# Projecting Q and K of the next head pair inside the attention loop, with two score regions instead of three

## The reference

```python
x = L0_attn_x                                     # (8, 2048, 1024) float32
x = x + attn(layernorm(x), W_qkv, W_out)
x = x + ffn(layernorm(x), w1, b1, w2, b2)

# attn: 16 heads of 64, W_qkv (16, 1024, 192), W_out (16, 64, 1024)
q, k, v = split(einsum('bsd,ndh->bnsh', x, W_qkv), 3)
attn = softmax(einsum('bnqh,bnkh->bnqk', q, k) / 8 + causal_mask)
out = einsum('bnqk,bnkh->bnqh', attn, v).reshape(B, -1, S)
return einsum('bds,nhd->bsd', out, W_out)         # 'h' and 'n' of W_out are summed away
# ffn: relu(x @ w1 + b1) @ w2 + b2, width 4096
```

## Time and profile before

| what | us |
|---|---|
| runs without the profiler | 1423.0 and 1475.0 (median 1449.0) |
| the profiled execution | 1413.5 |
| its span on the slowest core (core 7) | 1412.0 |
| spans of the other cores | 1388.7 to 1406.0 |
| mean granted clock of PE, by core | 0.886 to 0.898 of full |
| PE busy on core 7 | 1005.7 (71%) |
| DVE busy | 531.2 (38%) |
| ACT busy | 363.5 (26%) |
| eight head pairs, first QK matmul to last PV | about 608 |

### The profile page before, as it was taken

The page is one execution under the profiler, slowest core; times in us unless marked ns, Lnnn a source line. Parts: engine busy times, 40 slices in busy tenths (PEclk is TensorE's granted clock), DMA queues, the critical chain, the costliest instruction groups (busy, mean ns, idle before and its releaser), DMA issues.

```text
span 1412.0 us, 12665 instructions; the slowest of 8 cores (1388.7 to 1412.0 us)
## 1 busy us (share of the span) xinstructions
PE 1005.7 (71%) x4656; PEld 392.9 (28%) x4656; DVE 531.2 (38%) x686; ACT 363.5 (26%) x395; POOL 101.0 (7%) x131
## 2 busy tenths in 40 slices
PE   1155677758675866768575638798879887998797
PEld 0022332212221221212121113343334432443343
DVE  0545442362617162534536273222323232313301
ACT  0000007557392928464664700000000000000000
POOL 2100020000000000000000000111011101110110
PEclk9988998988798988989898859898999988999999
DMA  9900062010101000110002007879697949796976
GB/s 243 116 0 0 1 56 20 5 11 1 16 1 15 1 1 1 13 17 1 1 0 31 0 0 108 129 115 186 86 139 120 190 72 132 126 182 108 131 125 140
DMA packets 94331, 93.17 MB, mean 66 GB/s; under 512 B 40000, under 2 KB 72768, under 8 KB 94272
## 3 DMA queue, kind: packets, MB, share of 16 engines
q0 software_dynamic: 85248, 75.57, 38.6%
q1 hardware_dynamic: 9024, 16.80, 3.9%
HBM read 159.54 MB, written 8.39 MB: 119 GB/s over the span
## 4 chain that ended last, share of the span: by engine, by line
PE 60%; DVE 18%; DMA 12%; issue 4%; ACT 3%; DVEq 2%; POOL 0%; ACTq 0%; POOLq 0%
PE arena L667 16%; PE arena L622 12%; PE arena L478 11%; DMA wstage<-w 9%; PE arena L366 7%; PE arena L423 6%; PE arena L286 5%; DVE tmp_sb L550 4%; DVE oscr_sb L495 3%; DVE x_sb L561 3%; DMA wstage<-wout 2%; DVEq L51 2%; PE arena L438 2%; PE arena L239 1%; ACT p_sb L451 1%
## 5 line engine op out<-in xcount | busy, mean ns | idle before, releaser
L451 ACT ACTIVATE p_sb<-arena,cst_sb 128x1024 bf16<-128x1024 f32 (+1 forms) x320 | 288.9, 983 | 140.2 <-PE arena L438 134.0
L622 PE MATMUL arena<-lnf_sb,wstage 128*128 128x512 bf16 x1024 | 249.1, 408 | 64.0 <-DMA wstage<-w 53.6
L478 PE MATMUL arena<-p_sb,vaug_h 128*128 128x512 bf16 (+3 forms) x640 | 187.8, 378 | 131.8 <-DVE oscr_sb L495 96.2
L667 PE MATMUL arena<-w2stage,h_sb 128*128 128x512 bf16 x1024 | 221.7, 379 | 4.0 <-DVE h_sb L635 4.0
L635 DVE TENSOR_SCALAR h_sb<-arena,b1c_sb 128x512 bf16<-128x512 f32 x128 | 96.1, 751 | 215.0 <-PE arena L622 215.0
L622 PEld LDWEIGHTS arena<-lnf_sb,wstage 128*128 128x128 bf16 x1024 | 104.6, 103 | 207.6 <-issue 105.9
L366 PE MATMUL arena<-lnf_sb,wstage 128*128 128x512 bf16 x512 | 128.8, 412 | 36.8 <-DVE kpair L387 30.9
L667 PEld LDWEIGHTS arena<-w2stage,h_sb 128*128 128x128 bf16 x1024 | 99.9, 98 | 125.8 <-issue 5.9
L423 PE MATMUL arena<-qpair,kpair 64*128 64x512 bf16 (+3 forms) x640 | 123.0, 381 | 13.1 <-DVE kpair L387 13.1
L495 DVE COPY oscr_sb<-arena 128x512 f32<-128x512 f32 x64 | 44.3, 692 | 219.6 <-PE arena L478 214.7
L203 ACT ACTIVATE rsd_sb<-bag_sb,cst_sb 128x4 f32<-128x4 f32 x8 | 2.4, 300 | 457.1 <-DVE bag_sb L199 457.1
(11 more groups left out here) (37 smaller groups left out, 453.2 us busy)
## 6 DMA issues: line engine op xcount, KB each, us to landing
wstage<-w POOLq DMA_DIRECT2D x32, 1024.0 KB, 11.1
w2stage<-w POOLq DMA_DIRECT2D x64, 512.0 KB, 7.1
x_sb<-x SPq DMA_DIRECT2D x4, 2048.0 KB, 24.8
y<-y_sb SPq DMA_DIRECT2D x16, 512.0 KB, 6.5
wstage<-wqkv POOLq DMA_DIRECT2D x24, 256.0 KB, 12.3
wstage<-wout POOLq DMA_DIRECT2D x4, 512.0 KB, 21.2
b1c_sb<-b SPq DMA_DIRECT2D x32, 0.5 KB, 6.9
identb_sb<-identf POOLq DMA_DIRECT2D x1, 32.0 KB, 8.5
```

The costliest lines, as they stand in the source:

```text
L451: e.activation(AP(p_sb, (si_ % 3) * 1024, [[3 * 1024, 128], [512, 2], [1, w_]]), AP(arena, b_ + off_, [[AR, 128], [512, 2], [1, w_]]), AF. ...
L478: e.matmul(AP(arena, (4 + hx) * 512 + off_, [[AR, 128], [1, w_]]), vaug_h[:, hx, j_ * 128:(j_ + 1) * 128], AP(p_sb, (si_ % 3) * 1024 + hx ...
L622: (lambda s_, dc_, fb_, wp_: lambda e: e.matmul(bankap(fb_, TF), AP(wstage, s_ * 1024 + dc_ * 512 + wp_ * 128, [[8 * 1024, 128], [1, 128]] ...
L667: (lambda s_, ww_, c2_, dh_, t_: lambda e: e.matmul(bankap(t_, 512), h1_sb[:, ww_, 128 * c2_:128 * (c2_ + 1)], w2stage[:, s_, 512 * dh_:51 ...
```

## The change

Four things change, all in the attention stage.

- Q and K of pair n+1 are projected during the steps of pair n. `make_qk_chunks` cuts the projection into 8 chunks, each of 8 matmuls and two DVE copies. A chunk is added after PV(i) and its epilogue, where `npv % 5 == 2`: after PV(1), PV(6), PV(11), PV(16), PV(21), PV(26), PV(31) and PV(36). `qpair` and `kpair` have two halves, one for each parity of the pair. Only pair 0 is projected ahead of its own steps, as before.
- Banks 0 and 1 belong to the chunks alone. The scores have two regions instead of three, and the loop keeps two steps ahead instead of three. PE's queue in a pair is S(0), S(1), PV(0), S(2), PV(1), chunk, S(3), PV(2), and so on.
- The two V copies of a pair and the permute of the pair before now follow each other on DVE with nothing between them. The weight loads of a pair are issued one pair earlier.
- `onorm_sb` is bf16 instead of float32: written by L515, read by the strided multiply L550.

The core of the diff:

```diff
-        qpair = asb("qpair", [128, S], BF16)
-        kpair = asb("kpair", [128, S], BF16)
+        qpair = asb("qpair", [128, 2, S], BF16)
+        kpair = asb("kpair", [128, 2, S], BF16)
-        onorm_sb = asb("onorm_sb", [64, 2, S], F32)
+        onorm_sb = asb("onorm_sb", [64, 2, S], BF16)
...
-        s_reg_free = [("ex", 0)] * 3
-        REG_BASE = [1024, 3072, 0]
+        s_reg_free = [("ex", 0)] * 2
+        REG_BASE = [1024, 3072]
...
+        def make_qk_chunks(pi, slots_):
+            pr = pi % 2
+            chunks = []
+            for hix in range(2):
+                sl, dwqk = slots_[hix]
+                for g in range(4):
+                    def chunk(sl=sl, dwqk=dwqk, hix=hix, g=g):
+                        qb2 = g % 2
+                        mm_last = None
+                        for dcc in range(DC):
+                            w0 = ([dwqk, ("vv", vv_lnf1),
+                                   qk_bank_free[qb2]] if dcc == 0 else [])
...
+                        if g == 3:
+                            slot_free[sl] = ("mm", mm_last)
...
+                        qk_bank_free[qb2] = ("vv", vvk)
+                        vv_qk_pair[pi] = vvk
+                    chunks.append(chunk)
+            return chunks
...
+            if npair == 0:
+                for ch in make_qk_chunks(0, load_pair_slots(heads)):
+                    ch()
...
+            if npair + 1 < NH // 2:
+                next_chunks = make_qk_chunks(
+                    npair + 1,
+                    load_pair_slots((2 * npair + 2, 2 * npair + 3)))
+            else:
+                next_chunks = []
+            vv_qk_done = vv_qk_pair[npair]
             if pending_permute is not None:
                 perm_done = pending_permute()
                 pending_permute = None
...
-                reg = si % 3
+                reg = si % 2
...
             while npv < len(steps):
-                if nse < len(steps) and nse - npv < 3:
+                if nse < len(steps) and nse - npv < 2:
                     emit_se(nse)
                     nse += 1
                 else:
...
                     npv += 1
+                    if nck < len(next_chunks) and npv % 5 == 2:
+                        next_chunks[nck]()
+                        nck += 1
```

## The result

The changed kernel is slower. Its runs have a median of 1462.6 us (10 runs) against 1412.0 us for the kernel before (9 runs); the ratio is 1.035, with a 95% interval of 1.031 to 1.039. The prediction had 1441 on the profiled execution's scale, a ratio of 1.019, and put 1445 us on record. So the sign of its sum was right and its size was about half: +27 us forecast, +49 us by the ratio.

A forecast was written before the change was run, and what follows sets the result against it. The prediction took DVE to bound each pair's head and ACT its body. Its terms, -96.6 + 74 + 44 + 6 + 0 = +27 us on 1413.5, gave 1441, recorded as 1445 us on a 1418 scale, range 1415 to 1480.

The forecast's parts named there:

- Part 1: Head of each pair: without the QK block PV(4) starts earlier, 13.6 us in pairs 1 to 6, 15.0 in pair 7; -96.6 us.
- Part 2: Body: ACT idles about 1.6 us behind each exposed chunk, 10.3 us a pair in 7 pairs, 2 in pair 0; +74 us.
- Part 3: Body with two score regions: steps 1.13 us apart against 1.00 and costlier epilogues, 5.5 us a pair; +44 us.
- the walk of the prediction: Blocks 2 and 3 with two regions, summed link by link: 16.0 us against 14.6, and 20.5 against 17.1.
- Part 4: PE's clock: a half-clock stretch may follow the thin start of block 3; bounds 0 and 20, taken as +6 us.
- Part 5: onorm_sb in bf16: the permute's strided multiply L550 keeps its 1.89 us; 0 us, bounds -21 and +21.
- Rival A: Body: the chunks vanish in its slack, sum -40 us, 1378 us on the 1418 scale; chance 0.12.
- Rival C: PE's clock: half clock at the start of the three blocks behind an epilogue, +60 us instead of 6, 1499; chance 0.08.

The follow-up runs named there:

- a_nochunk: The changed kernel with pairs 0 and 1 projected up front and the later pairs' projections left out; 1397.4 us, ratio 0.986.
- b_two_fill: b_two with 6 matmuls that nobody reads behind each of PV(11), PV(12), PV(23) and PV(24); 1477.1 us, ratio 1.043.
- b_two: The kernel before with two score regions and two steps ahead, nothing else changed; 1505.3 us, ratio 1.063.
- a_both: The changed kernel with the permute spread behind two epilogues and chunks placed in PE's waits, two ahead of PV(0); 1299.9 us, ratio 0.916.
- b_spread: The kernel before with the permute moved out of the head, half behind each epilogue of blocks 1 and 2; 1355.1 us, ratio 0.954.
- a_both_la3: a_both with three steps ahead of the PV matmuls instead of two; 1241.8 us, ratio 0.874.

## Why the prediction was wrong, step by step

The prediction added up five parts. Its sum was +27 us, and measured were +49 by the ratio and +51.3 in spans. The term that failed is that of the two regions, Parts 3 and 4: forecast 50 us, measured 85 to 93.

**Part 1, the head: right.** Forecast 13.6 us in pairs 1 to 6 and 15.0 in pair 7. From copy to copy it is 13.6 to 14.8 in pairs 1 to 6 (34.6 - 20.9 = 13.7 in pair 5) and 15.1 in pair 7 (35.0 against 19.9), together 99.5 against the 96.6 forecast.

**Part 2, the chunks: the mechanism right, the price a sixth too high.** Forecast 10.3 us a pair in the body and 1.4 in the head; measured against `a_nochunk`, 8.5 and 1.4 in pair 5, and 8.9 in the blocks on average. The idle of 1.62 us behind a chunk is as forecast. Block 3 costs the forecast 4.8. The difference is mostly in block 2 (2.0 against 3.2), where the chunk behind PV(11), forecast as free, also keeps the clock up: 1.00 with chunks, 0.81 in `a_nochunk`.

**Part 3, two regions: the step that failed, in block 1.** In `b_two_fill` the clock is 1.00 in blocks 2 and 3, so it shows the walk of the prediction without the clock: 16.1 and 20.6 us, where the walk gave 16.0 and 20.5. For block 2 the 14.6 that it was compared with was the wrong base, for it held a stretch at the low clock. Against the 13.6 of the even pairs the chain costs 2.4 us and not 1.4. Block 1 was not walked. The prediction gave it +0.7, with the argument that PE is the bound there in both kernels. Over eight pairs it is 13.4 us in `b_two` against 10.3, +3.1; in pair 5 it is +3.4. The changed kernel's timeline shows what the argument missed:

```profile
560.44 1.01 PE L504 MATMUL arena<-p_sb,vaug_h 128*128 128x512 bf16 x2 [9.04 <-DVE oscr_sb L521]
561.39 0.61 PE L449 MATMUL arena<-qpair,kpair 64*128 64x512 bf16 x2
561.51 1.15 ACT L533 ACTIVATE rec_sb<-rec_sb,cst_sb 64x1024 f32<-64x1024 f32 x1
562.57 2.09 ACT L477 ACTIVATE p_sb<-arena,cst_sb 128x1024 bf16<-128x1024 f32 x2
...
563.81 1.01 PE L504 MATMUL arena<-p_sb,vaug_h 128*128 128x512 bf16 x2 [1.81 <-ACT p_sb L477]
```

With two steps ahead only exp(4) is in ACT's queue when block 0's epilogue is added; exp(5) stands behind the logarithm and the exponential of the row sums. In the 9 us of the stall ACT could have done it, but its queue was held by the epilogue. So PV(5) starts 3.4 us after PV(4), where it was 1.5 before. It is the same lost exponential that the prediction counted in block 3. `b_two` has the same 3.4 us, which makes 1.9 of the 3.4 of its pair 5.

The other 1.5 us come behind PV(5), and there the clock differs. The kernel before, whose first 5 us behind PV(4) are in the earlier trace rows (PE busy 4.97 of them), is at full clock from 614.5 on. `b_two` is at half clock 5 us longer, after a stretch with PE busy 3.16 of 5 us:

```profile
614.50:618.00 3.50, 3.50 (x26) 1.24 (x24) 0.00 (x0) 3.20 (x5) 0.00 (x0) 1.00 0.00 0
```

```profile
669.50:674.50 5.00, 3.16 (x9) 0.61 (x10) 1.29 (x2) 4.17 (x4) 0.00 (x0) 0.50 0.00 0
674.50:679.50 5.00, 5.00 (x20) 1.32 (x19) 0.00 (x0) 3.15 (x4) 0.00 (x0) 0.53 0.00 0
```

No experiment holds block 1 alone at full clock in `b_two`. The nearest are `a_both` (two steps ahead, two chunks in the waits, 11.5 us at 1.00) and `b_spread` (three steps ahead, 9.6 us at 1.00 in pair 5). They are 1.9 us apart, which fits a delay of 1.9 at PV(5) and the low clock for the rest. In any case PE was not the bound all through block 1, as the argument had it: with two steps ahead it waits 1.81 us for exp(5). Missed: 2.4 us x 8 = 19 us.

**Part 4, the clock: mis-sized for the two-region loop.** Forecast +6, with bounds of 0 and 20. The filling brings blocks 2 and 3 of `b_two` down by 25.5 us over eight pairs (426.0 to 400.5 for all blocks), 1.6 in each block. Some 4 us of such loss, the 1.0 in four block 2s, were in the time before, so the clock's net cost is about 21 us in these two blocks, at the upper bound. The fault is the reasoning that one such stretch a pair was already in the time before: it was there in about every second pair, and two regions make one at the start of block 2 and one of block 3. In the changed kernel the chunk in block 2 saves the one, and block 3 has the other:

```profile
592.00:597.00 5.00, 2.19 (x10) 0.46 (x8) 2.22 (x4) 3.70 (x5) 0.00 (x0) 0.71 0.01 3
597.00:602.00 5.00, 4.17 (x13) 1.31 (x14) 1.07 (x2) 2.80 (x3) 0.00 (x0) 0.61 0.00 0
602.00:619.00 17.00, 14.81 (x75) 4.65 (x72) 4.14 (x6) 11.75 (x12) 0.87 (x1) 1.00 0.00 0
```

Parts 3 and 4 together: forecast 50 us. In `b_two` the blocks are longer by 3.1 + 3.5 + 4.9 us a pair, 93 us over eight pairs (89 by the ratio), and in `a_nochunk` 85 us (418.5 against 333.3).

The Trainium skill, "TensorE: Matmul & The Clock Gate", table "Why this matters for your kernels", advises to leave no long idle gaps between bursts of matmuls. The trace agrees in direction, and adds that two shorter ones in a row did it in `b_two`: 1.47 and 2.45 us, with one step's work between them.

**Part 5, bf16: right.** Forecast 0, measured ratio 0.999. The rule weighed there is that of the Trainium skill, "Vector Engine (DVE) Microarchitecture Reference", section 5.2. It gives its higher price for hops of 24 words on both sources or on the destination; carried over to 16-word hops on one source, it made an estimate of 25 us. The measured 1.87 us against 1.89 shows no such cost here.

**The sum.** In spans the change is +51.3 us (1463.3 against 1412.0). From copy to copy the heads give -99.5. The blocks of pairs 1 to 6 give +115.1, those of pair 7 +10.8 and of pair 0 +21.9. The first copy of pair 0 comes 3.9 us later, 2.1 of it because the first QK matmul starts later. That makes +52, and the other stages, which were not changed, give back 1. Against the forecast, the two regions are 35 us over their 50 (by `a_nochunk`), the chunks 10 under their 72 in the blocks, and the heads 3 better. So two smaller misses happened to cover a third of the large one. A pair came to 81.8 us, where about 79 was forecast.

**Chances and scale.** The prediction put 0.48 on slower, 0.42 on no change. With the measured 3.1 us for block 1 in Part 3, the sum would have been +46 and the matter clear. It also placed its time on 1418, between 1413.5 and 1423, while the median then shown was 1449, drawn up by one of the two runs; more runs put the kernel before at 1412. The 1445 on record is thus 2.3% above the 1412 of the kernel before, but below the 1449 that it was given with: read against that, it says no change, though the sum behind it says slower. Rival A fell: the exponentials don't run on through a chunk. Rival C, the clock that falls behind each epilogue, was the live one, but it came with the two-region loop: in `b_two` the three blocks of pair 5 have 0.58, 0.80 and 0.85, and in the changed kernel the chunk in block 2 brings that block to 1.00.

**What stays open.** Why two regions with three steps ahead still lose 4.8 us a pair: PE's waits at a taken region and the clock that falls behind them weren't taken apart. How the 3.1 us of block 1 divide between the lost exponential and the clock is shown only by comparing different kernels.

## What to carry to other kernels

Before cutting a lookahead, walk every block that begins behind an epilogue, the one under a long stall too. In an in-order queue the depth decides which work stands ahead of the epilogue, and that is lost even where the engine seems to have time. Filler work that is to hide must be placed in the waits that the profile names and not at even distances: the same chunks cost about 70 us more at each fifth step than behind the epilogues. Do the interleaving last: it paid clearly once the chunks stood in the waits and the DVE work was out of the head (0.916), and more with the scores again issued further ahead of PV (0.874).

## What the hardware showed unexpectedly

More matmuls made the kernel faster. With 192 more of them, nobody's input, `b_two_fill` beats `b_two` by 28 us, the ratios being 1.043 and 1.063, because PE at full clock then does the wanted matmuls in half the time (PV 0.59 us instead of 1.01).

In `b_two` the clock fell behind a stretch in which PE was busy 1.18 of 5 us, none of its gaps longer than 2.5 us; in `b_two_fill` PE was busy 3.66 us of the same stretch and the clock stayed at 1.00. The clock can also be low where nothing shows: block 0 ran at half clock under the permute, and that became a cost only when the permute was gone.

Less work can even cost time. In `a_both_la3` pair 7 carries no chunks, and it takes 57.2 us where pairs 2 to 6, with eight chunks each, take 51.4. Its clock is 0.76 against 1.00:

```profile
578.16:635.37 57.21, 42.10 (x189) 11.57 (x190) 23.92 (x26) 45.87 (x48) 0.00 (x0) 0.76 0.00 1
```
